# A four-stage transformer kernel on one core: the norms take the next group's scales earlier, and the experts' weight loads wait for the first two tiles' rows

## The chip, the cores and the metric

The kernel runs on one core of a Trainium2 chip, as one program in one launch. The metric is the time of one execution on the device in microseconds (us), lower is better. The kernel before took 1563.83 us (median of three runs, 1562.64 to 1567.59).

## What is computed

The input x is 4 x 512 tokens of width 256. Four layers follow one another, each adding its result to x: attention, a mixture of experts, a state space layer, and the same mixture of experts again. All start with a norm over the 256 features.

```python
def _layernorm(x, axis=-1, eps=1e-05):
    m = jnp.mean(x, axis=axis, keepdims=True)
    v = jnp.var(x, axis=axis, keepdims=True)
    return (x - m) / jnp.sqrt(v + eps)
...
x = x + attention(_layernorm(x))
x = x + ffn(_layernorm(x))
x = x + state_space(_layernorm(x))
x = x + ffn(_layernorm(x))
...
gate_weights = jax.nn.softmax(x @ Wg + bg); topv, topi = jax.lax.top_k(gate_weights, 2)   # 8 experts
h = gelu(x @ W1[n] + b1[n]); h = gelu(h @ W2[n] + b2[n]); eo = h @ W3[n] + b3[n]          # 512, 512, 256 wide
out = sum over the two experts n of a token of topv * eo
```

## The kernel before, in words

x stays in the on-chip memory (SBUF) as X, 16 blocks of 128 tokens. Each layer is made of stages; a stage is one block of five engine programs with a barrier at its end, so a stage can start only when every engine has finished the one before. Inside a stage the order of work on an engine is the order of the code, and the engines meet through semaphores. Float32 products are made of three float16 products (high x high, high x low, low x high, lines 115 to 117), so every operand is first split into a high and a low half.

**Two of the four norms** (before attention, stage "ln0", and before the state space layer, stage "ln2") are made by layer_norm_stage. They run over G = 4 groups of four blocks. For a group g, VectorE takes the statistics (lines 182 to 187), ScalarE the root (line 223), VectorE the reciprocal, the shift and one of the four normalised blocks (normalise, lines 191 to 198), ScalarE the other three blocks (line 232), TensorE turns the group with eight transposes (line 262), ScalarE copies the high half (line 238, copy_turned) and VectorE subtracts the low half (line 204, low_turned). "alongside" is other work put between: in ln0 the splitting of the attention's weights, ScalarE line 144 and VectorE line 149; in ln2 a few steps on ScalarE (line 1494) and most of it on GpSimd (lines 1502 and 1505). Before the change VectorE's loop runs, for each g: normalise(g), statistics(g + 2), low_turned(g - 1), alongside(g).

**The mixture of experts** (ffn_stage, run twice, "ffn1" and "ffn2") makes its own norm and the routing, and then walks over 24 tiles, 15 of 256 rows and 9 of 128 rows, each of one expert. The rows of a tile are gathered from memory by GpSimd with one indirect DMA for 128 rows (line 1033); xs_loaded[0] counts those of even tiles, xs_loaded[1] those of odd tiles, 16 for each DMA, so that 32 means the two gathers of a wide tile. Gathers 0 and 1 (two DMAs each) are started as soon as the row numbers are there (from_ready). The weights of a tile are 2 MB in split form (W); eight tiles' weights fit at once. SyncE asks for them in the order of tiles: for tile 0 in two parts, W1 (512 KB, line 1000, semaphore first_in) and the rest (1.5 MB, line 1001), then one load for each tile (line 1003); from tile 8 on a load waits until tile j - 8 is done (y_psum). The first eight tiles' weights are therefore asked for within 10 us of the start.

TensorE (lines 1110 to 1177) begins with: transpose tile 0's rows (line 1116), layer 1 of tile 0, transpose tile 1's rows; then for each tile layer 2, the next tile's layer 1, the transposes of the tile after that, and layer 3. Layer 1 of tile 0 waits for first_in and for the split rows; layer 2 of tile 0 waits for the 1.5 MB; layer 1 of tile j waits for tile j's 2 MB.

Of the kernel before, what the change touches and what calls it, by code (L numbers as in the profile page):

```python
# [155 lines left out]
def layer_norm_stage(nc, stage, X, XTh, XTl, identf, make_alongside):  # L156

    G = NT // TB  # L160
    with ExitStack() as ctx:
        t = Tensors(nc, ctx, stage)
        stats, mv = t.sb("stats", [P, NT, 6]), t.sb("mv", [P, NT, 2])
        sd, rs, shift = t.sb("sd", [P, NT]), t.sb("rs", [P, NT]), t.sb("shift", [P, NT])
        ring = t.sb("ring", [P, 2, TB, D])
        alongside = make_alongside(t)
        bank = t.banks()
        ordered = t.sem("ordered")
        var_ready, sd_ready, scale_ready = t.sem("var_ready"), t.sem("sd_ready"), t.sem("scale_ready")
        norm_dve, norm_act = t.sem("norm_dve"), t.sem("norm_act")  # L170
        xpose_ready, high_ready, low_ready = (t.sem(n) for n in ("xpose_ready", "high_ready", "low_ready"))
        block = t.block()
        tok = lambda g: slice(g * S, (g + 1) * S)
        tiles_of = lambda g: slice(g * TB, (g + 1) * TB)

        @block.vector
        def _(dve):
            link = Chain(dve, ordered)

            def statistics(g):  # L180
                for n in range(g * TB, g * TB + TB):
                    last = dve.bn_stats(stats[:, n, :], X[:, n, :])
                link(last)
                for n in range(g * TB, g * TB + TB):
                    last = dve.bn_aggr(mv[:, n, :], stats[:, n, :])
                link(last)
                dve.tensor_scalar(mv[:, tiles_of(g), 1], mv[:, tiles_of(g), 1], EPS, None, ALU.add).then_inc(var_ready, 1)

            def normalise(g):
                dve.wait_ge(sd_ready, g + 1)  # L190
                link(dve.reciprocal(rs[:, tiles_of(g)], sd[:, tiles_of(g)]))
                dve.scalar_tensor_tensor(shift[:, tiles_of(g)], mv[:, tiles_of(g), 0], -1.0, rs[:, tiles_of(g)], ALU.mult,
                                         ALU.mult).then_inc(scale_ready, 1)
                if g >= 2:

                    dve.wait_ge(xpose_ready, KD * (g - 1))
                n = g * TB
                dve.tensor_scalar(ring[:, g % 2, 0, :], X[:, n, :], mv[:, n, 0:1], rs[:, n:n + 1], ALU.subtract,
                                  ALU.mult).then_inc(norm_dve, 1)

            def low_turned(g):
                for k in range(KD):
                    dve.wait_ge(high_ready, g * KD + k + 1)
                    dve.tensor_tensor(XTl[:, k, tok(g)], bank[g % 2 * KD + k][:, :], XTh[:, k, tok(g)],
                                      ALU.subtract).then_inc(low_ready, 1)

            statistics(0)
            statistics(1)
            for g in range(G):
                normalise(g)  # L210
                if g + 2 < G:
                    statistics(g + 2)
                if g >= 1:
                    low_turned(g - 1)
                alongside.vector(dve, g)
            low_turned(G - 1)
            alongside.vector(dve, G)

        @block.scalar
        def _(act):  # L220
            def root(g):
                act.wait_ge(var_ready, g + 1)
                act.activation(sd[:, tiles_of(g)], mv[:, tiles_of(g), 1], ACT.Sqrt).then_inc(sd_ready, 1)

            def normalise(g):
                act.wait_ge(scale_ready, g + 1)
                if g >= 2:

                    act.wait_ge(xpose_ready, KD * (g - 1))
                for i in range(1, TB):  # L230
                    n = g * TB + i
                    last = act.activation(ring[:, g % 2, i, :], X[:, n, :], ACT.Identity, scale=rs[:, n:n + 1], bias=shift[:, n:n + 1])
                last.then_inc(norm_act, 1)

            def copy_turned(g):
                for k in range(KD):
                    act.wait_ge(xpose_ready, g * KD + k + 1)
                    act.activation(XTh[:, k, tok(g)], bank[g % 2 * KD + k][:, :], ACT.Copy).then_inc(high_ready, 1)

            root(0)  # L240
            root(1)
            for g in range(G):
                normalise(g)
                if g + 2 < G:
                    root(g + 2)
                if g >= 1:
                    copy_turned(g - 1)
                alongside.scalar(act, g)
            copy_turned(G - 1)
            alongside.scalar(act, G)  # L250

        @block.tensor
        def _(pe):
            for g in range(G):
                pe.wait_ge(norm_dve, g + 1)
                pe.wait_ge(norm_act, g + 1)
                if g >= 2:

                    pe.wait_ge(low_ready, KD * (g - 1))
                for k in range(KD):  # L260
                    for i in range(TB):
                        ins = pe.transpose(bank[g % 2 * KD + k][:, i * P:(i + 1) * P], ring[:, g % 2, i, k * P:(k + 1) * P],
                                           identf[:, :])
                    ins.then_inc(xpose_ready, 1)

        @block.sync
        def _(sp):
            alongside.sync(sp)

        @block.gpsimd  # L270
        def _(pool):
            alongside.gpsimd(pool)
# [601 lines left out]
def ffn_stage(nc, stage, ins, X, split_w, xn_rows, y_rows, row_moves, c, out):  # L874
# [6 lines left out]
    G, C = NT // TB, UNITS  # L881
    PAIR = TOPK * NT
    identf = c["identf"]
    with ExitStack() as ctx:
# [56 lines left out]
        xs_loaded, y_stored = row_moves  # L941
# [13 lines left out]
        def units_of(j, par):  # L955

            return sum(units(i) for i in range(par, j + 1, 2))
# [9 lines left out]
        def expert_of(eng, j):  # L967

            return eng.value_load(tile_expert[0:1, j:j + 1], min_val=0, max_val=NE - 1)

        def tile_weights(j):

            return W[:, j % NE * 2 * WCOLS:(j % NE + 1) * 2 * WCOLS]
# [4 lines left out]
        @block.sync  # L978
        def _(sp):
            sp.dma_start(wg[:, :, :], ins["L0_ffn_Wg"].rearrange("(k p) n -> p k n", p=P)).then_inc(loaded, 16)  # L980
            sp.dma_start(bg[:, :], ins["L0_ffn_bg"].unsqueeze(0).broadcast_to([P, NE])).then_inc(loaded, 16)

            for g in range(G):
                sp.wait_ge(norm_dve, g + 1)
                sp.wait_ge(norm_act, g + 1)
                sp.dma_start(packed_rows(xn_rows[1:, :], g), XN[:, g * TB:(g + 1) * TB, :]).then_inc(xn_stored, 16)
            for layer in range(2):
                sp.dma_start(b12[:, layer, :], ins[f"L0_ffn_b{layer + 1}"].rearrange("e (m p) -> p (e m)", p=P),
                             allow_slow_non_contiguous=True).then_inc(biases, 16)
            sp.dma_start(b3b[:, :, :], ins["L0_ffn_b3"].unsqueeze(0).broadcast_to([P, NE, D])).then_inc(biases, 16)  # L990
            sp.wait_ge(tiles_ready, 1)
            for j in range(NTILE):
                src = split_w[ds(expert_of(sp, j), 1), :, :].rearrange("e p n -> p (e n)")
                if j >= NE:

                    sp.wait_ge(y_psum, j - NE + 1)
                if j == 0:
                    halves = lambda a: a.rearrange("p (x n) -> p x n", x=2)
                    to, src = halves(tile_weights(0)), halves(src)
                    sp.dma_start(to[:, :, 0:W2_AT], src[:, :, 0:W2_AT]).then_inc(first_in, 16)  # L1000
                    sp.dma_start(to[:, :, W2_AT:], src[:, :, W2_AT:]).then_inc(weights[0], 16)
                else:
                    sp.dma_start(tile_weights(j), src).then_inc(weights[j % NE], 16)

            for par in range(2):
                sp.wait_ge(y_stored[par], 16 * units_of(NTILE - 1, par))
            for k, g in BACK:
                sp.dma_start(back[:, k * G + g, :, :], packed_rows(y_rows[1 + k * B * S:, :], g)).then_inc(back_loaded[k * G + g], 16)
# [1331 lines left out]
```

## Time and profile before

| | |
|---|---|
| time, median of 3 runs | 1563.83 us (1562.64 to 1567.59) |
| the profiled execution's own time | 1557.24 us |
| its span from first to last instruction | 1555.5 us |
| TensorE busy | 1230.6 us, 79% of the span |
| VectorE busy | 1003.2 us, 64% |
| ScalarE, GpSimd busy | 617.3 and 621.2 us, 40% each |
| mean granted TensorE clock | 0.897 |
| stage ln0 | from 11.3 to 39.3 us |
| expert loop of ffn1: first gather | 483.07 us |
| stage ln2 | from 741.9 to 766.0 us |
| expert loop of ffn2: first gather | 1293.34 us |

Times of day in the text are us from the start of the span. The 40 slices of the page, in tenths, show TensorE near full through attention and both expert loops, and short valleys at the norms and routings:

```profile
PE   1789898989844999994456869888888846999992
PEclk8799999999965999997578968999999966999997
```

The second line is the TensorE clock granted, in tenths. An execution is a row of stages, so a stretch in which TensorE stands still in a valley goes straight into the time, while a stretch in which another engine waits inside an expert loop doesn't.

### The profile page before, as it was taken

The page shows a single profiled execution, that of the slowest core. Times are in us where ns is not written, and L with a number is a line of the kernel's source. Part 1 is how long each engine was busy: PE and PEld are TensorE (multiplying, and loading weights), DVE is VectorE, ACT ScalarE, POOL GpSimd, SP SyncE. Part 2 cuts the span into 40 slices and gives each one's busy share as a digit, 9 for nine tenths or more (in the row PEclk, how much of TensorE's full clock was granted, in tenths as well). Part 3 has the DMA queues.
Part 4 walks back from the last instruction along what each step waited for, and adds up shares of the span by engine and source line. Part 5 has one row for each costly group of instructions (what it writes and reads, how often), then busy time and mean ns, then how long its engine had stood idle before and what let it go on. Part 6 is the DMA issues. An engine that isn't in the chain of part 4 may idle for free. (4 is left out here: it accounts for less than half of the span.)

```text
span 1555.5 us, 35259 instructions
## 1 busy us (share of the span) xinstructions
PE 1230.6 (79%) x13688; PEld 936.0 (60%) x13688; DVE 1003.2 (64%) x2108; ACT 617.3 (40%) x1380; POOL 621.2 (40%) x540
## 2 busy tenths in 40 slices
PE   1789898989844999994456869888888846999992
PEld 1356665656533989883223436666666634898882
DVE  5478898888865555465586555766666465554565
ACT  4357676666641333342455631121111132333341
POOL 0245445454502333232304345775757502333322
PEclk8799999999965999997578968999999966999997
DMA  4656656666425976643100000000000036967634
GB/s 147 146 136 160 182 166 159 175 162 168 126 60 221 421 289 234 249 163 122 54 1 14 1 14 2 2 3 2 3 2 2 2 83 271 421 247 257 220 142 172
DMA packets 93701, 209.89 MB, mean 135 GB/s; under 512 B 33058, under 2 KB 64547, under 8 KB 87395
## 3 DMA queue, kind: packets, MB, share of 16 engines
q1 hardware_dynamic: 83938, 185.11, 36.4%
q0 software_dynamic: 7488, 20.46, 3.8%
q8 instruction: 109, 1.79, 0.5%
q10 hardware_dynamic: 2112, 2.10, 0.4%
q14 instruction: 54, 0.43, 0.1%
HBM read 152.84 MB, written 37.49 MB: 122 GB/s over the span
## 5 line engine op out<-in xcount | busy, mean ns | idle before, releaser
L1221 ACT ACTIVATE ffn_h<-ffn_bank,ffn_b 128x256 f32<-128x256 f32 (+1 forms) x384 | 144.7, 431 | 271.7 <-PE ffn_bank L117 268.6
L2190 POOL TENSOR_TENSOR ssm_GL<-ssm_L,ssml_G 128x512 f32<-128x512 f32 x128 | 164.9, 1298 | 109.5 <-DVE ssm_L L2099 109.5
L1398 DVE CAST ffn_hh<-ffn_h 128x512 f16<-128x512 f32 (+1 forms) x192 | 73.1, 381 | 185.9 <-ACT ffn_h L1221 185.1
L1033 POOL DMA_INDIRECT ffn_xs<-xn_rows,ffn_from_rows x78 | 78.5, 1007 | 271.2 <-PE ffn_bank L1116 184.7
L115 PE MATMUL ffn_bank<-ffn_hh,ffn_W 128*128 128x256 f16 (+1 forms) x768 | 180.2, 253 | 5.2 <-DVE ffn_hl L1400 5.0
L116 PE MATMUL ffn_bank<-ffn_hl,ffn_W 128*128 128x256 f16 (+1 forms) x768 | 180.0, 252 | 0.0
L117 PE MATMUL ffn_bank<-ffn_hh,ffn_W 128*128 128x256 f16 (+1 forms) x768 | 180.0, 252 | 0.0
L1955 PE MATMUL ssm_Y<-ssm_GL,ssmh_windows 64*32 64x64 f32 x4096 | 145.9, 224 | 8.6 <-POOL ssm_GL L2190 8.2
L2099 DVE TENSOR_TENSOR_SCAN ssm_L<-ssm_bank,ssmh_ident 128x512 f32<-128x512 f32 x128 | 151.2, 1209 | 1.7 <-PE ssm_bank L1938 1.6
L1955 PEld LDWEIGHTS ssm_Y<-ssm_GL,ssmh_windows 64*32 64x32 f32 x4096 | 125.0, 111 | 37.4 <-issue 25.8
L641 ACT ACTIVATE att_prob<-att_bank,att_nmax 128x512 f32<-128x512 f32 (+3 forms) x256 | 127.4, 526 | 29.8 <-DVE att_nmax L723 28.5
L730 DVE TENSOR_TENSOR att_ptl<-att_bank,att_pth 128x384 f16<-128x384 f32 (+1 forms) x192 | 114.0, 594 | 33.9 <-ACT att_pth L648 33.8
L2029 ACT ACTIVATE ssmh_windows<-ssml_dtx 128x64 f32<-128x64 f32 x128 | 32.7, 256 | 259.3 <-PE ssm_Y L1955 255.6
L648 ACT ACTIVATE att_pth<-att_bank 128x384 f16<-128x384 f32 (+1 forms) x192 | 101.5, 529 | 76.7 <-PE att_bank L588 76.7
L588 PE MATMUL att_bank<-main_identf,att_prob 128*128 128x128 f32 x640 | 99.2, 280 | 34.4 <-ACT att_prob L641 19.7
L1040 POOL DMA_INDIRECT y_rows<-ffn_y,ffn_to_rows x78 | 77.1, 988 | 122.3 <-DVE ffn_y L1409 87.0
L723 DVE TENSOR_REDUCE att_nmax<-att_bank 128x1 f32<-128x512 f32 (+3 forms) x256 | 117.6, 479 | 10.6 <-PE att_bank L578 10.3
L833 POOL TENSOR_TENSOR att_rope<-att_turned 128x512 f32<-128x512 f32 x36 | 45.7, 1269 | 193.4 <-DVE att_turned L768 134.9
L1400 DVE TENSOR_TENSOR ffn_hl<-ffn_h,ffn_hh 128x512 f16<-128x512 f32 (+1 forms) x192 | 113.8, 593 | 6.6
L588 PEld LDWEIGHTS att_bank<-main_identf,att_prob 128*128 128x128 f32 x640 | 71.8, 143 | 55.4 <-ACT att_prob L641 41.3
L115 PE MATMUL ffn_bank<-ffn_xTh,ffn_W 128*128 128x256 f16 (+1 forms) x384 | 92.4, 257 | 3.4 <-DVE ffn_xTl L1391 3.4
L116 PE MATMUL ffn_bank<-ffn_xTl,ffn_W 128*128 128x256 f16 (+1 forms) x384 | 92.3, 257 | 0.0
(348 smaller groups left out, 3186.3 us busy)
## 6 DMA issues: line engine op xcount, KB each, us to landing
ffn_W<-split_w SPq DMA_DIRECT2D x46, 2048.0 KB, 10.4
att_piece<-in_ffn_w SPq DMA_DIRECT2D x32, 512.0 KB, 5.4
split_w<-att_halves SPq DMA_DIRECT2D x32, 512.0 KB, 4.4
att_Q<-att_pair SPq DMA_DIRECT2D x64, 128.0 KB, 2.4
ffn_back<-y_rows SPq DMA_DIRECT2D x16, 512.0 KB, 7.2
att_KB<-att_krl SPq DMA_DIRECT2D x8, 512.0 KB, 5.5
att_Q<-att_pair SPq DMA_DIRECT2D x64, 64.0 KB, 2.1
xn_rows<-ffn_XN SPq DMA_DIRECT2D x8, 512.0 KB, 2.6
```

The lines of the kernel that those rows point to most:

```text
L115: pe.matmul(out, ah, bh, start=start, stop=False)
L116: pe.matmul(out, ah, bl, start=False, stop=False)
L117: return pe.matmul(out, al, bh, start=False, stop=stop)
L588: ins = pe.transpose(bk[:, j * P:(j + 1) * P], prob[:, g % 2, at + j * P:at + (j + 1) * P], identf[:, :])
L641: ins = act.activation(prob[:, g % 2, p_at[i]:p_at[i] + n], bank[bk][:, at:at + n], ACT.Exp, bias=nmax[:, g % 2, i:i + 1])
L723: ins = dve.tensor_reduce(nmax[:, g % 2, i:i + 1], bank[bk][:, at:at + (i + 1) * P], AX.X, ALU.max, negate=True)
L730: dve.tensor_tensor(ptl[:, g % 2, at:at + n], bank[5 + (3 * g + c) % 2][:, 0:n], pth[:, g % 2, at:at + n], ALU.subtract).then_inc(pT_low, 1)
L1221: ins_ = act.activation(h[layer][:, m, 0:n], bank[1 + 2 * layer + u][:, (m % 2) * n:(m % 2 + 1) * n], ACT.Gelu, bias=bias[:, ds(e + m, 1)])
L1400: dve.tensor_tensor(hl[layer][:, half, 0:n], h[layer][:, half, 0:n], hh[layer][:, half, 0:n], ALU.subtract).then_inc(h_low[layer], 1)
L1955: ins = pe.matmul(Y[out_rows, q // 2 * 2 + par, q % 2, i, :], windows[rows, p % WINDOWS, x, i, at:at + GROUP], GL[rows, p % RING, x, i, :] ...
L2099: dve.tensor_tensor_scan(flat(L[:, p % RING, :, :, :]), bank[p % 2][:, :], ident8[:, :], 0.0, ALU.mult, ALU.add).then_inc(scan_done, 1)
L2190: pool.tensor_tensor(GL[:, p % RING, :, :, :].rearrange("p x i n -> p x (i n)"), L[:, p % RING, :, :, :].rearrange("p x i n -> p x (i n)") ...
```

## The change

It has two parts. In layer_norm_stage VectorE normalises group 0 ahead of its loop and then, in the turn of g, group g + 1, after the statistics of g + 2 and ahead of low_turned(g - 1) and of the work alongside. ScalarE, TensorE, SyncE and GpSimd keep their programs. In the expert loops SyncE waits for both gathers of tile 0 before it asks for the 1.5 MB of tile 0's weights, and for both gathers of tile 1 before it asks for tile 1's weights and those of later tiles. No other DMA, wait or instruction is added or removed.

```diff
             statistics(0)
             statistics(1)
+            normalise(0)
             for g in range(G):
-                normalise(g)
                 if g + 2 < G:
                     statistics(g + 2)
+                if g + 1 < G:
+                    normalise(g + 1)
                 if g >= 1:
                     low_turned(g - 1)
                 alongside.vector(dve, g)
...
                     sp.dma_start(to[:, :, 0:W2_AT], src[:, :, 0:W2_AT]).then_inc(first_in, 16)
+                    sp.wait_ge(xs_loaded[0], 32)
                     sp.dma_start(to[:, :, W2_AT:], src[:, :, W2_AT:]).then_inc(weights[0], 16)
+                    sp.wait_ge(xs_loaded[1], 32)
                 else:
                     sp.dma_start(tile_weights(j), src).then_inc(weights[j % NE], 16)
```

## Rows read from the trace of the kernel before

**Rows 1.** Waits of TensorE over the whole span: us in total, times, longest

```profile
PE ln_bank L262 <- ACT ln_ring L232: 67.5, 8, 29.9
PE ffn_bank L1116 <- DMA ffn_xs<-xn_rows,ffn_from_rows: 18.2, 2, 9.2
```

**Rows 2.** Timeline of ln0: start, duration, engine, line, what [idle before <- releaser]

```profile
21.11 1.29 DVE L204 TENSOR_TENSOR attw_XTl<-ln_bank,attw_XTh 128x512 f16<-128x512 f32 x2 [0.76 <-ACT attw_XTh L238]
...
23.39 2.29 DVE L149 TENSOR_TENSOR attw_wrl<-ln_staged,attw_wrh 128x2048 f16<-128x2048 f32 x1 [1.00 <-ACT attw_wrh L144]
25.60 2.29 DVE L149 TENSOR_TENSOR attw_wtl<-ln_staged,attw_wth 128x2048 f16<-128x2048 f32 x1
...
28.20 1.58 ACT L232 ACTIVATE ln_ring<-main_X,ln_shift,ln_rs 128x256 f32<-128x256 f32 x3 [3.05 <-DVE ln_shift L192]
...
30.30 1.29 DVE L204 TENSOR_TENSOR attw_XTl<-ln_bank,attw_XTh 128x512 f16<-128x512 f32 x2 [1.81 <-ACT attw_XTh L238]
...
31.83 1.36 DVE L149 TENSOR_TENSOR attw_wxl<-ln_staged,attw_wxh 128x1152 f16<-128x1152 f32 x1 [0.25 <-ACT attw_wxh L144]
...
36.20 1.29 DVE L204 TENSOR_TENSOR attw_XTl<-ln_bank,attw_XTh 128x512 f16<-128x512 f32 x2 [1.81 <-ACT attw_XTh L238]
```

**Rows 3.** Timeline of ln2, the rows that decide its end

```profile
749.67 6.00 POOL L1502 TENSOR_TENSOR ssml_zs<-ssml_zs 128x1344 f32<-128x1344 f32 x2 [16.70 <-DMA ssml_zs<-in_L_attn_b_mup_vector]
...
750.78 1.94 DVE L187 TENSOR_SCALAR ln_mv<-ln_mv 128x4 f32<-128x4 f32 x1
...
754.89 0.80 DVE L192 SCALAR_TENSOR_TENSOR ln_shift<-ln_mv,ln_rs 128x4 f32<-128x4 f32 x1
...
755.73 1.58 ACT L232 ACTIVATE ln_ring<-main_X,ln_shift,ln_rs 128x256 f32<-128x256 f32 x3 [1.79 <-DVE ln_shift L192]
...
759.43 1.58 ACT L232 ACTIVATE ln_ring<-main_X,ln_shift,ln_rs 128x256 f32<-128x256 f32 x3
...
763.26 2.73 POOL L1505 TENSOR_TENSOR ssmi_wil<-ssml_zs,ssmi_wih 128x1344 f16<-128x1344 f32 x1 [0.95 <-ACT ssmi_wih L1494]
```

**Rows 4.** Timeline of the start of the expert loop in ffn1

```profile
484.08 0.67 SPq L1000 DMA_DIRECT2D ffn_W<-split_w  x1
...
484.52 0.95 POOL L1033 DMA_INDIRECT ffn_xs<-xn_rows,ffn_from_rows  x1 [0.30 <-issue]
...
491.46 1.09 PE L1116 MATMUL ffn_bank<-main_identf,ffn_xs 128*128 128x128 f32 x4 [9.18 <-DMA ffn_xs<-xn_rows,ffn_from_rows]
...
494.23 0.37 PE L115 MATMUL ffn_bank<-ffn_xTh,ffn_W 128*128 128x256 f16 x1 [1.69 <-DVE ffn_xTl L1391]
...
501.60 0.27 PE L115 MATMUL ffn_bank<-ffn_hh,ffn_W 128*128 128x256 f16 x1 [1.92 <-DVE ffn_hl L1400]
...
506.83 0.27 PE L115 MATMUL ffn_bank<-ffn_xTh,ffn_W 128*128 128x256 f16 x1
```

**Rows 5.** Line 1033, 483 to 483.5 us: issue to landing of gather one

```profile
DMA to landing us min/median/max: 3.1/3.1/3.1
```

**Rows 6.** Line 1033, 484.4 to 485 us: the same of gather two

```profile
DMA to landing us min/median/max: 6.8/6.8/6.8
```

**Rows 7.** Line 1033, 487 to 487.5 us: the same of gather four

```profile
DMA to landing us min/median/max: 7.9/7.9/7.9
```

**Rows 8.** Gather queue (q0): packets, MB, share; 487 to 488, then 488 to 489

```profile
q0 software_dynamic: 2, 0.01, 5.6%
...
q0 software_dynamic: 20, 0.07, 31.7%
```

**Rows 9.** DMA issues 483 to 500 us: size, issue to landing

```profile
ffn_W<-split_w SPq DMA_DIRECT2D x1, 1536.0 KB, 10.7
```

**Rows 10.** Line 1003, tile 1's load alone, at 486.3 us: issue to landing

```profile
DMA to landing us min/median/max: 14.9/14.9/14.9
```

**Rows 11.** Line 1003, all 46 loads of 2 MB: issue to landing

```profile
DMA to landing us min/median/max: 8.1/10.4/41.7
```

**Rows 12.** Busy time 494.2 to 498.8: PE, PEld, DVE, ACT, POOL, PE clock, DMA share, GB/s

```profile
494.20:498.80 4.60, 4.57 (x22) 3.21 (x23) 0.00 (x0) 1.72 (x3) 0.81 (x1) 0.50 1.00 417
```

## The prediction

> **What bounds the kernel now.** I read the page's busy times and slices first: TensorE is busy for 79% of the span and close to full inside attention and the expert loops, so nothing that another engine does there can shorten the whole unless TensorE is kept waiting. The waits of TensorE say where it stands still. Two entries belong to this change. In the two reordered norms it waits 67.5 us for the normalised blocks, of which 29.9 us is one wait that begins before ln2 [rows 1]; and for the gathered rows at the start of an expert loop it waits 18.2 us, 9.2 at most, two times in all [rows 1], once in ffn1 and once in ffn2. The timelines of these three places then show which engine's work ends last there. In ln0 it is VectorE: it works without pause but for the gaps in brackets, the second low half starts at 30.30 and the third at 36.20, each after 1.81 us of idleness [rows 2]. In ln2 it is the pair of ScalarE and GpSimd, whose last product starts at 763.26 and takes 2.73 us [rows 3]. At the start of the expert loop it is the second gather: issued at 484.52, and TensorE's transposes begin at 491.46 [rows 4, 6].
>
> **Part 1, ln0: 4.5 us off.** Nothing is added or removed; normalise(2) and normalise(3) move ahead of low_turned(0) with the weights' split behind it, and of low_turned(1) with its split. normalise(1) has the same place as before, so all is unchanged up to VectorE's fourth statistics. There VectorE idles 0.76 us before the first low half at 21.11 [rows 2]. normalise(2), 0.7 us of small operations on VectorE, goes into that gap: 0.62 us gained, as 0.14 is left. The two big splits follow; the wait of 1.00 us before 23.39 is for ScalarE's first split [rows 2], which is not moved, so it stays. The second split starts at 25.60 and ends about 27.8. ScalarE meanwhile has had the scales of group 2 since 21 us and need not idle its 3.05 us before 28.20 [rows 2]: it normalises group 2 right after its own splits, at about 25.1 to 26.6, and copies group 1's high half by 27.6. VectorE does normalise(3) at 27.8 and finds that high half ready at 28.4: the gap of 1.81 before 30.30 goes. The 0.25 before 31.83 goes too, as ScalarE has the next split done at 28.7 and VectorE comes at 29.6. TensorE turns group 2 at 26.7 to 28.7, ScalarE normalises group 3 behind its small splits from 29.2 and copies group 2's high half by 31.7, and VectorE, busy to 31.5, goes on without the second 1.81, before 36.20 [rows 2]. What is late next is VectorE's own work, with no gap of note left; TensorE's turn of group 3, 30.8 to 32.7, and the copies to 33.4 are just in time. Sum: 0.62 + 1.81 + 0.25 + 1.81 = 4.49, all of it on the path, since the barrier waits for the last low half. The bounds are 3.0, if the copies of group 3 come a step late, and 4.8.
>
> **Part 1, ln2: nothing.** The same move, but here GpSimd runs two products of 6.00 us together from 749.67 on, 3.0 each [rows 3]. VectorE's little addition of the fourth group, which takes 0.17 us elsewhere, was held for 1.94 us from 750.78, to the end of the first product, and its shift for 0.80 from 754.89, to the end of the second at 755.67 [rows 3]. In the new order normalise(2) comes right behind that addition, at 752.7, when the second product has just begun. Its reciprocal can run but its shift would be held to 755.7, exactly where it ends today; ScalarE's blocks start at 755.73 again [rows 3] and the low half of group 0 is pushed from 753.5 to 756.0, ready at 757.3, when TensorE needs it. Group 3's blocks on ScalarE have no idle time ahead of them at 759.43 [rows 3]: ScalarE was busy with the weights, so earlier scales change nothing. I take 0; the bounds are 0.3 lost and, if the shift slips in before the second product, the 1.79 us that ScalarE idles before 755.73 [rows 3]. The Trainium skill (SBUF — State Buffer, "Who interferes with whom") says that VectorE and GpSimd share a pair of ports, that a VectorE instruction with two SBUF inputs or in a two-port mode takes it, and that whoever issues first keeps it for its whole instruction while the other blocks. The two stretched rows agree; a norm that was free of this rule would give the 1.79.
>
> **Part 2, the expert loops: 2.2 us off each.** Today SyncE asks for 512 KB at 484.08 and, 0.9 us later, for 1.5 MB, and then tile 1's weights at 486.3, while GpSimd issues four gathers 1.2 us apart. The first gather landed 3.1 us after its issue, the second 6.8, the fourth 7.9 [rows 5 to 7]. The second sets when TensorE begins. What of its 3.7 extra us goes away? The wait takes the 1.5 MB and all behind it out of its way, but not the 512 KB. Of the gathers' packets 2 moved from 487 to 488 and 20 from 488 to 489 [rows 8]; so the second gather hardly moved until 3.5 us after its issue, while the 512 KB were in the engines, and I leave that delay in. From then on it shared the engines with the 1.5 MB up to 491.3. Alone, with its descriptors written, it should need no more than the 1.9 us that the first gather took from the end of its instruction (1.2 of the 3.1) to landing [rows 5]. So it lands between 488.8 and 489.7, I take 489.1: 2.2 us. The bounds are 0 (the sharing was not the cause) and 3.7 (the second is as fast as the first). The transposes, the split and layer 1 move with it: layer 1 then starts at 492.0 instead of 494.23, layer 2 at 499.4 instead of 501.60, tile 1's layer 1 at 504.6 instead of 506.83 [rows 4]. ffn2's rows are the same within 0.3 us at all these places, so 2 x 2.2 = 4.4.
>
> **What the new waits hold.** Behind them on SyncE's queue are the weight loads only. The 1.5 MB are issued at 489.2 instead of 484.9. Lag today is 10.7 us with the 512 KB ahead and tile 1's load behind [rows 9]; a load of 2 MB took 8.1 at best and 10.4 in the median [rows 11]. So it lands between 497 and 499.9, against a need at 499.4: cover of about 2 us, at worst 0.5 short. The second wait ends when gather four lands: it was issued at 487.0, and with the engines free of the 1.5 MB until about 490.7 it lands at 490 to 491; at worst at its present 494.9 [rows 7]. Tile 1's load follows 0.8 us later (the read of its expert's number), at 491.5, and lands by the 8.1 to 10.4 at 499.6 to 501.9, behind the 1.5 MB for some of it, against a need at 504.6. Later tiles need theirs 10.9 us apart and the queue delivers one in about 5. So the waits are hidden, with a cover of some 3 us that the present order doesn't need. The Trainium skill (DMA: Bandwidth & Descriptors, "Anatomy of one DMA") speaks against such waits: a DMA costs about 2.0 us fixed, mostly completion, plus its bytes at 436 GB/s, and a wait on a completion exposes the fixed part. By it the 1.5 MB would take 5.6 us and tile 1's load 6.8, which is an estimate from that page and would land both in time.
>
> **The clock.** Layer 1 of tile 0 runs at a granted clock of 0.50, which is 1.2 GHz, after TensorE stood for 9.2 us [rows 12, 1], with 22 products in 4.6 us. It idles 7 us instead and I expect it to be as slow. When the clock rises against the work can shift by a couple of us at either start and at attention's; at half speed half of that is lost or won. I put 1 us on either side.
>
> **Sum.** 4.5 + 0 + 4.4 = 8.9 us. The profiled execution would go from 1557.24 to 1548.3. It was 6.6 us faster than the median of the runs, 0.4%, which is an offset of the run and not of the kernel, so I take the saving from the median: 1563.8 - 8.9 = 1554.9, or 0.57% less.
>
> **Rivals.** (a) More: the second gather becomes as fast as the first, 2 x 3.7, and ln2 gives its 1.8: 13.7 us, 1550.1. For it: the engines had room from 487 to 488, so something other than the 512 KB may have held the second gather, and that would be the 1.5 MB's descriptors. Against: the packets of rows 8. Chance 0.15. (b) The sharing costs the gather little. DMA engines move 417 GB/s in all [rows 12], 26 each, so one 6 KB packet costs 0.23 us, and the gather has three or so packets in each engine: 0.7 us if it waits for one of them each time. Then the loops give 0 to 0.7 each and the sum is 4.5 to 5.9: 1559.3 to 1557.9. The Trainium skill (DMA: Bandwidth & Descriptors, "Queues, rings and completion order") says that each engine goes round robin between its queues, packet by packet, which is this case. Against: a gather in the loads' shadow took 6.8 to 7.9 and not 3.8. Chance 0.2. (c) ln0 doesn't follow, as the copies of groups 2 and 3 come late and half of it is lost: 2 us less, 1557. Chance 0.05. (d) Slower: the second wait ends only at 494.9 and tile 1's load then takes today's 14.9 us [rows 10], landing at 510.6 against 504.6; TensorE waits 6.0, less the 2.2 gained, so 3.8 lost in each loop, 7.6 less ln0's 4.5: 3.1 slower, 1566.9. It decides from the point where tile 1's weights land later than 506.8, 15.3 us after an issue at 491.5. Against: the 14.9 hold the 512 KB and the 1.5 MB that are ahead of it, which by then are done or nearly. Chance 0.04. That the change does nothing at all would need both (b) and (c), and is in them.
>
> **How the numbers follow.** The forecast has a chance of 0.56, 1553 to 1557 by its own bounds. The range takes in (a), (b) and (c), with 1 us for the clock and 1.5 for the medians: 1549.5 to 1562. A difference of 0.3%, 4.7 us, is about what a measurement here can tell from none. The forecast, (a), (c) and the upper half of (b) are faster by more: 0.79; the rest of (b), with some runs of (c), is 0.17; slower by more than that is only part of (d) and a bad clock: 0.04.
>
> **What the new profile would show.** In ln0: no gap before VectorE's low halves but the first and the one before the big split, ScalarE without its 3.05 us, the stage's end at 34.8 in place of 39.3. In ln2: ScalarE's third group at 755.7 less the shift of the start, and the end unmoved. In the loops: TensorE's wait for the gather down from 9.2 to 7, the second gather's lag from 6.8 to 4.6, no idle time before layer 2 of tile 0 or layer 1 of tile 1 put down to a weight load. A lag of 6 or more, or a wait for ffn_W, would prove me wrong; a lag near 3 would be (a).

## The result, and the profile after

| | before | after |
|---|---|---|
| median, six runs each | 1563.75 us (1562.64 to 1567.59) | 1555.84 us (1552.65 to 1559.88) |
| ratio | | 0.9948, 95% interval 0.9931 to 0.9965 |
| the profiled execution's own time | 1557.24 us | 1555.88 us |
| its span | 1555.5 us | 1554.1 us |
| mean granted TensorE clock | 0.897 | 0.901 |

The change takes 7.9 us off, 0.52% with an interval of 0.35 to 0.69%; 8.9 had been forecast. The two profiled executions differ by 1.4 us only. That is not the change's worth: the profile of before was a short execution of its kernel, and the last section says what made it short. So the places are compared first, and the sums after.

On the page of after the busy times and slices look as they did (lines of TensorE and of its granted clock, in tenths). A saving of half a per cent can't be seen here:

```profile
PE   2698898989745999994346869888888846999992
...
PEclk9899999999965999997578968999999966999996
```

TensorE's waits, the answer to [rows 1] (us in total, times, longest), show both parts of the change at once. The normalised blocks cost 62.5 us instead of 67.5, with ln2's 30 among them as before, and the gathers 13.7 instead of 18.2:

```profile
PE ln_bank L264 <- ACT ln_ring L234: 62.5, 8, 30.0
...
PE ffn_bank L1120 <- DMA ffn_xs<-xn_rows,ffn_from_rows: 13.7, 2, 7.2
```

**ln0**, the timeline of after (start, duration, what, [idle before <- releaser]), the answer to [rows 2]:

```profile
21.14 1.29 DVE L204 TENSOR_TENSOR attw_XTl<-ln_bank,attw_XTh 128x512 f16<-128x512 f32 x2 [0.16 <-ACT attw_XTh L240]
...
23.42 2.29 DVE L149 TENSOR_TENSOR attw_wrl<-ln_staged,attw_wrh 128x2048 f16<-128x2048 f32 x1 [1.00 <-ACT attw_wrh L144]
25.08 1.57 ACT L234 ACTIVATE ln_ring<-main_X,ln_shift,ln_rs 128x256 f32<-128x256 f32 x3
...
28.44 1.28 DVE L204 TENSOR_TENSOR attw_XTl<-ln_bank,attw_XTh 128x512 f16<-128x512 f32 x2
...
31.50 1.28 DVE L204 TENSOR_TENSOR attw_XTl<-ln_bank,attw_XTh 128x512 f16<-128x512 f32 x2
...
33.30 1.28 DVE L204 TENSOR_TENSOR attw_XTl<-ln_bank,attw_XTh 128x512 f16<-128x512 f32 x2
...
35.29 0.59 PE L115 MATMUL att_bank<-attw_XTh,attw_wxh 128*128 128x512 f16 x1 [2.59 <-PEq L76]
```

The gap of 0.76 before VectorE's first low half is 0.16, the 1.00 before the big split stands, and the low halves at 28.44 and 31.50 start with no idle time where there were 1.81 us each. ScalarE does group 2's blocks at 25.08 with none of its 3.05 us. Attention's first product comes at 35.29 instead of 39.99.

**ln2**, the answer to [rows 3]. What VectorE gained in place it lost again while GpSimd's products ran:

```profile
750.25 6.00 POOL L1506 TENSOR_TENSOR ssml_zs<-ssml_zs 128x1344 f32<-128x1344 f32 x2 [16.53 <-DMA ssml_zs<-in_L_attn_b_mup_vector]
...
751.13 2.17 DVE L187 TENSOR_SCALAR ln_mv<-ln_mv 128x4 f32<-128x4 f32 x1
...
753.41 2.85 DVE L192 SCALAR_TENSOR_TENSOR ln_shift<-ln_mv,ln_rs 128x4 f32<-128x4 f32 x1
...
756.29 1.58 ACT L234 ACTIVATE ln_ring<-main_X,ln_shift,ln_rs 128x256 f32<-128x256 f32 x3 [1.78 <-DVE ln_shift L192]
```

The shift, 0.16 us elsewhere, takes 2.85 and ends with GpSimd's second product, at 756.25; ScalarE idles 1.78 us before the third group, as it idled 1.79. From ln2's first transpose to the state space layer's first product it is 21.10 us, against 20.93. Over all the profiles below whose GpSimd products are whole, the mean is 21.0 us in six of the new order and 21.1 in six of the old.

**The start of the expert loop in ffn1**, the answer to [rows 4] (SPq are SyncE's requests):

```profile
483.36 0.67 SPq L1002 DMA_DIRECT2D ffn_W<-split_w  x1
483.81 0.95 POOL L1037 DMA_INDIRECT ffn_xs<-xn_rows,ffn_from_rows  x1 [0.30 <-issue]
...
488.80 1.08 PE L1120 MATMUL ffn_bank<-main_identf,ffn_xs 128*128 128x128 f32 x4 [7.24 <-DMA ffn_xs<-xn_rows,ffn_from_rows]
488.82 0.58 SPq L1004 DMA_DIRECT2D ffn_W<-split_w  x1
...
490.30 7.10 SPq L1007 DMA_DIRECT2D ffn_W<-split_w  x7
...
491.57 0.37 PE L115 MATMUL ffn_bank<-ffn_xTh,ffn_W 128*128 128x256 f16 x1 [1.69 <-DVE ffn_xTl L1395]
...
498.97 0.10 PEld L115 LDWEIGHTS ffn_bank<-ffn_hh,ffn_W 128*128 128x128 f16 x1 [2.74 <-DMA ffn_W<-split_w]
499.00 0.37 PE L115 MATMUL ffn_bank<-ffn_hh,ffn_W 128*128 128x256 f16 x1 [2.53 <-DVE ffn_hl L1404]
```

The second gather is issued at 483.81 and TensorE starts on its rows at 488.80, 5.0 us later, where it was 6.9 [rows 4]. The 1.5 MB are asked for at 488.82 and have landed when layer 2 wants them. The weight load at 498.97 is put down to that DMA and the product 0.03 us behind it to VectorE, because the weight load itself waits for nothing but the DMA. By the semaphores' times in the trace the last part of the 1.5 MB landed at 498.10, and VectorE finished at 498.86. So VectorE ended the wait, and the load had 0.8 us to spare.

### The profile page after: what moved, and what is told of

It is laid out like the page before. It is cut to its first block and busy times, and to the rows that moved or that the text cites. A ratio compares the mean times of both kernels' runs of the same rounds, so it can differ in the third digit from the quotient of the medians.

```text
span 1554.1 us, 35259 instructions
## 1 busy us (share of the span) xinstructions
PE 1234.1 (79%) x13688; PEld 936.3 (60%) x13688; DVE 1006.2 (65%) x2108; ACT 616.6 (40%) x1380; POOL 621.4 (40%) x540
## 3 DMA queue, kind: packets, MB, share of 16 engines
q8 instruction: 109, 1.79, 0.5%
```

## The experiments

All of them are set against the kernel before on the same chip. Times of after's and before's profiles scatter by some us in attention, so single places are read in the profiles and kernels are compared by ratios. Each ratio is followed by its 95% interval.

### The norms alone

```diff
+            normalise(0)
             for g in range(G):
-                normalise(g)
                 if g + 2 < G:
                     statistics(g + 2)
+                if g + 1 < G:
+                    normalise(g + 1)
```

> The norms' new order alone, no new waits in the expert loops. My theory: ln0 ends 4.5 us earlier and ln2 gives nothing, because VectorE's shift of group 2 is held by GpSimd's second product (2 to 3 us in its row); the gathers keep their 6.8 us lag. Time 4.5 us less than before (ratio 0.997). Rival one, that the norms carry the whole saving: 8 us less. Rival two, that later stages give ln0's saving back, since TensorE's clock in attention falls more often when it starts earlier: 0 to 1 us less.

Measured: 1558.97 us against 1562.39, 0.9966 (0.9951 to 0.9981), which is 5.3 us. Its ln0 took 17.94 us from the first transposes to attention's first product, before's 22.68.

### Both waits alone, the first alone, the second alone

```diff
                     sp.dma_start(to[:, :, 0:W2_AT], src[:, :, 0:W2_AT]).then_inc(first_in, 16)
+                    sp.wait_ge(xs_loaded[0], 32)
                     sp.dma_start(to[:, :, W2_AT:], src[:, :, W2_AT:]).then_inc(weights[0], 16)
+                    sp.wait_ge(xs_loaded[1], 32)
```

> The two waits of SyncE alone, the norms in their old order. My theory: the second gather lands 4.7 to 5.0 us after its issue in place of 6.8, TensorE's wait for the rows falls from 18.2 to about 13.7 us over both loops, and the time is 4.4 us less (ratio 0.997), with 1 us either way from when the clock rises. Rival, that the late loads or the clock take it back (a wait for ffn_W, or a fall to 1.2 GHz inside layer 1 or 2 of tile 0): the same wait for the rows, but 0 to 1.5 us less.

> Only the first wait: the 1.5 MB of tile 0 wait for tile 0's rows, tile 1's load follows at once; norms in their old order. My theory: tile 0's rows land as with both waits, since all that shares with them is behind the first wait, so TensorE's wait for the rows is about 13.7 us in all and the time is as in the kernel with both waits, 4.4 us less; gathers three and four may land later by 1 to 3 us, which costs nothing because TensorE asks for them 7 us later. Rival, that holding tile 1's load back is what helps: no better than before.

> Only the second wait: the 1.5 MB are asked for at once as before, tile 1's load and those behind it wait for tile 1's rows; norms in their old order. My theory: the 1.5 MB alone share with the second gather, whose lag stays at 6.5 to 6.8 us, and the time is that of the kernel before within 1 us. Rival, that the number of loads queued behind matters (descriptors of several loads being made while the gather's are fetched): lag 5 to 6 us and 1 to 3 us less.

Measured: both 0.9972 (0.9959 to 0.9985), the first 0.9973 (0.9958 to 0.9988), the second 0.9997 (0.9982 to 1.0011); in us 4.4, 4.2 and 0.5. TensorE's wait for the gathers in the profiles of the two waits, of the first and of the second:

```profile
PE ffn_bank L1118 <- DMA ffn_xs<-xn_rows,ffn_from_rows: 13.9, 2, 7.1
```

```profile
PE ffn_bank L1117 <- DMA ffn_xs<-xn_rows,ffn_from_rows: 14.4, 2, 7.4
```

```profile
PE ffn_bank L1117 <- DMA ffn_xs<-xn_rows,ffn_from_rows: 18.5, 2, 9.6
```

All three came as the first theory of each had it. What follows: the loops' gain is the first wait's. The second neither gives nor costs anything that can be told. The norms' 5.3 and the waits' 4.4 add up to 9.7, against 7.9 to 8.6 of the whole change; the intervals, some 2 us either way each, cover that.

### Before once more, and GpSimd's second product in ln2 cut to 8 columns, in the new order and in the old

```diff
-            pool.tensor_tensor(self.w[:, k, :], self.w[:, k, :], self.mup, ALU.mult).then_inc(self.scaled, 1)
+            n = PROJ if k == 0 else 8
+            pool.tensor_tensor(self.w[:, k, 0:n], self.w[:, k, 0:n], self.mup[:, 0:n], ALU.mult).then_inc(self.scaled, 1)
```

> The kernel before once more, for a second profile of it. In the first one attention took 401.7 us from its first to its last product, and the step from tile 17's transposes to tile 18's took 5.9 us in both expert loops; in the kernel after these are 405.8 us and 7.2 us. One theory: both are luck of an execution and not of the change, so a second profile shows attention anywhere from 401 to 407 us and the step at 7.2. The other: the old order keeps them short, so it shows 401.7 and 5.9 again.

> The kernel after with GpSimd's second product in ln2 cut from 1344 to 8 columns, which leaves the state space layer's second half of scaled weights out of the computation. My theory: VectorE's shift of group 2, 2.85 us long in the kernel after, falls to 0.2, and ScalarE's blocks of group 2 start 1.2 to 1.8 us earlier, right behind its copy. Rival: the shift is slow for a reason of its own (its operands), stays over 1 us, and nothing moves.

> The kernel before with the same cut (the second half of the scaled weights of the state space layer is left out of the computation). Beside the run above it shows what the new order of the norm is worth in ln2 when nothing holds VectorE: from ln2's first transposes to its last, 0.6 to 1.8 us less in the new order. If the order is worth nothing there at all, both take the same.

Both kernels leave out the scaling of the other columns of the second half. Measured, one execution each: 1552.45 us in the new order, 1562.13 in the old; single executions scatter too much for these two times to be compared, so the timelines are read. The two products together now take 3.19 us in place of 6.00. In the new order:

```profile
749.28 3.19 POOL L1507 TENSOR_TENSOR ssml_zs<-ssml_zs 128x1344 f32<-128x1344 f32 x2 [16.43 <-DMA ssml_zs<-in_L_attn_b_mup_vector]
750.27 2.06 DVE L187 TENSOR_SCALAR ln_mv<-ln_mv 128x4 f32<-128x4 f32 x1
...
752.45 0.16 DVE L192 SCALAR_TENSOR_TENSOR ln_shift<-ln_mv,ln_rs 128x4 f32<-128x4 f32 x1
```

In the old order:

```profile
759.20 0.16 DVE L192 SCALAR_TENSOR_TENSOR ln_shift<-ln_mv,ln_rs 128x4 f32<-128x4 f32 x1
759.39 1.58 ACT L232 ACTIVATE ln_ring<-main_X,ln_shift,ln_rs 128x256 f32<-128x256 f32 x3 [1.15 <-DVE ln_shift L192]
```

The addition is still held to the end of the first product, which was left as it was, and the shift is not held any more: 2.85 us became 0.16 with nothing else in the code changed. From ln2's first transpose to the state space layer's first product it took 19.08 us in the new order and 20.32 in the old, where it was 21.1 with whole products in both. So without the second product the new order would be worth 1.2 us here, by one profile each. It is GpSimd's product that holds VectorE's shift, and it takes about what the change could give in ln2. The Trainium skill (SBUF — State Buffer, "Who interferes with whom") has the rule that of VectorE and GpSimd the one that issues first keeps the shared ports for its whole instruction and the other blocks. The trace agrees with it: with the product there the shift ended when the product did, and without it the shift took 0.16 us.

Before's second profile took 1553.94 us, 3.3 less than its first, with the same code. Its two waits for the gather were 8.07 and 7.96 us. Its attention took 400.69 us and its step from tile 17 to tile 18 took 5.9, as the expectation's second theory had it. That the old order keeps them short was disproved only by later profiles: the run with the cut product in the old order had an attention of 406.00, and before's third profile, below, had 406.07 and a step of 7.1.

### The 512 KB behind the first two gathers as well

```diff
+                    sp.wait_ge(xs_loaded[0], 32)
                     sp.dma_start(to[:, :, 0:W2_AT], src[:, :, 0:W2_AT]).then_inc(first_in, 16)
-                    sp.wait_ge(xs_loaded[0], 32)
                     sp.dma_start(to[:, :, W2_AT:], src[:, :, W2_AT:]).then_inc(weights[0], 16)
```

> The kernel after with the 512 KB of W1 asked for behind the first wait too, so that no weight load runs beside tile 0's gathers. My theory: the 512 KB cost the second gather 1.3 to 1.8 us, so its lag falls from 4.9 to 3.1 to 3.5 us, but W1 then lands 4 to 5 us after that, at about the time at which layer 1 starts now or 1 us later: the same time as the kernel after, within 1.5 us. Rival, that the 512 KB cost it nothing and the second gather is late from its own making: lag still 4.5 or more, layer 1 waits for W1, 2 to 4 us slower than the kernel after.

Measured: 1557.74 us against 1560.9, 0.9981 (0.9963 to 0.9999): 0.0033 worse than after's 0.9948, some 5 us. The timeline of the start in ffn1:

```profile
483.57 0.95 POOL L1037 DMA_INDIRECT ffn_xs<-xn_rows,ffn_from_rows  x1 [0.30 <-issue]
...
486.40 1.09 PE L1120 MATMUL ffn_bank<-main_identf,ffn_xs 128*128 128x128 f32 x4 [5.08 <-DMA ffn_xs<-xn_rows,ffn_from_rows]
486.45 0.67 SPq L1003 DMA_DIRECT2D ffn_W<-split_w  x1
...
493.23 0.39 PE L115 MATMUL ffn_bank<-ffn_xTh,ffn_W 128*128 128x256 f16 x1 [5.74 <-DMA ffn_W<-split_w]
```

and one line of its DMA issues there (size, us to landing):

```profile
ffn_W<-split_w SPq DMA_DIRECT2D x1, 512.0 KB, 6.7
```

The expectation of the same time within 1.5 us missed, although its mechanism on the gather's side came out: 2.8 us from issue to TensorE's start, the time of a gather with no weight load beside it. So of before's 6.9 us in ffn1 the 1.5 MB and what follows took 1.9 and the 512 KB 2.2; by the means over all profiles, 6.45 without the first wait, 4.77 with it and 2.86 here, they took 1.7 and 1.9. The loss is on the other side. The expectation gave the 512 KB 4 to 5 us. SyncE asked for them 0.85 us ahead of the 1.5 MB, and they took 6.7 us, where after's, asked for early, took 5.0. Layer 1 starts 11.1 us after the first gather's issue (482.12), against a mean of 9.0 in the loops with the first wait alone or with both, about 2 us later in each loop; that is 4 of the 5. The 5 compares ratios of two chips and is good to some 4 us either way.

### The 512 KB between the first gather and the second

Two profiles had then shown both ends: asked for early the load slows the gather, asked for late it is late itself. The next kernel gives the first gather a semaphore of its own, and SyncE waits for that one gather before the 512 KB; TensorE waits for both semaphores.

```diff
+        rows0 = xs_loaded[2]
...
+                    sp.wait_ge(rows0, 16)
                     sp.dma_start(to[:, :, 0:W2_AT], src[:, :, 0:W2_AT]).then_inc(first_in, 16)
-                    sp.wait_ge(xs_loaded[0], 32)
+                    sp.wait_ge(xs_loaded[0], 16)
...
-                                            ).then_inc(xs_loaded[j % 2], 16)
+                                            ).then_inc(rows0 if n == 0 else xs_loaded[j % 2], 16)
```

> The kernel after once more, beside the three below on one chip. By the sum of its parts (norms 0.9966, waits 0.9972) the ratio should be 0.994 and by its first timing 0.9948: 8 to 9 us less than before. If attention really runs some 3 us longer when it starts 4.7 us earlier (405.6 to 406.7 us in four profiles of the new order, 400.7 to 406.8 in six of the old one), its profile shows 405 or more again; if that was luck, 401 to 407.

> The kernel after with the 512 KB of W1 held until the first gather has landed (it gets a semaphore of its own). My theory: the second gather's lag falls from 4.9 to 3.0 to 3.7 us, W1 lands 5.0 to 5.5 us after its issue, which is 0.7 to 1.2 us before layer 1 starts now, so 1.5 to 2.4 us less than the kernel after over both loops (ratio to it 0.9985 to 0.999). Rival: W1 lands 6.7 us after its issue as when all loads waited, so layer 1 starts where it does now or 0.5 us later and nothing is gained.

> The norms' new order alone, once more. Theory one: ln0's 4.7 us arrive in full, ratio 0.997, and attention's length in the profile is as scattered as in the old order (401 to 407 us). Theory two: attention gives 2 to 4 us of it back, ratio 0.9985 to 0.9995, with attention at 405 us or more in the profile once more.

> The kernel before, a third profile, to see how attention scatters in the old order and whether the step from tile 17's to tile 18's transposes (5.9 or 7.2 us) goes by the occasion and not by the kernel. If it goes by the occasion it is the same here as in the other kernels of this call.

| on one chip | median us | against before |
|---|---|---|
| after, again | 1554.66 | 0.9945 (0.9929 to 0.9961) |
| the 512 KB later | 1552.88 | 0.9935 (0.9918 to 0.9952) |
| the norms alone, again | 1557.02 | 0.9967 (0.9951 to 0.9982) |
| before, its third profile | 1564.39 (one execution) | (median of the runs 1563.19) |

The start in ffn1 with the 512 KB later:

```profile
479.38 0.95 POOL L1039 DMA_INDIRECT ffn_xs<-xn_rows,ffn_from_rows  x1 [0.30 <-issue]
...
481.08 0.67 SPq L1004 DMA_DIRECT2D ffn_W<-split_w  x1
...
482.24 1.09 PE L1124 MATMUL ffn_bank<-main_identf,ffn_xs 128*128 128x128 f32 x4 [5.10 <-DMA ffn_xs<-xn_rows,ffn_from_rows]
482.26 0.58 SPq L1006 DMA_DIRECT2D ffn_W<-split_w  x1
...
486.03 0.39 PE L115 MATMUL ffn_bank<-ffn_xTh,ffn_W 128*128 128x256 f16 x1 [2.70 <-DMA ffn_W<-split_w]
...
489.24 17.61 SPq L1009 DMA_DIRECT2D ffn_W<-split_w  x8
```

TensorE waits 5.1 us for the gather, no more than with the 512 KB out of the way, and then for the 512 KB, whose wait is 2.70 where VectorE alone would have made it 1.69. Layer 1 starts 8.1 us after the first gather's issue (477.94) in ffn1 and 8.35 in ffn2, against 9.2 and 8.5 in after and 8.8 and 8.6 in after again, so it is 1.1 us sooner at best and 0.1 at least. The gather's lag of 2.9 us to TensorE's start and the 512 KB's 4.9 and 5.2 are close to what the theory had. The median is 1.8 us below after's, also as forecast, but the intervals overlap: that this kernel beats before is shown, that it beats after isn't. It pays elsewhere: tile 1's load is asked for only at 489.24, which fits gathers three and four sharing the DMA engines with the 1.5 MB now (not tested apart), and in ffn2 tile 1's layer 1 had to wait for its weights:

```profile
1299.94 7.00 SPq L1009 DMA_DIRECT2D ffn_W<-split_w  x7
...
1311.43 0.28 PE L115 MATMUL ffn_bank<-ffn_xTh,ffn_W 128*128 128x256 f16 x1 [2.23 <-DMA ffn_W<-split_w]
```

That 2.23 us is the mechanism of the prediction's rival (d), the late second wait, met in a neighbour of this kernel. The profile shows no gain after it: from ffn2's first transpose to the end of the span it took 297.6 us against 294.1 in after again, and what made this profile the shorter one is its attention, 401.44 us against 406.29.

## Why the prediction came out right, and where its sizes were off

**ln0, right.** Forecast 4.49 us in four pieces (0.62, 1.81, 0.25, 1.81), measured 4.70 at attention's first product. VectorE and ScalarE came where the working put them: blocks of group 2 at 25.08 (25.1 said), TensorE's turns at 26.75 and 30.77 (26.7 and 30.8), the last low halves ending at 34.58. That no copy of groups 2 and 3 came late disposes of rival (c). It arrives in full: the norms alone gave 0.9966 and 0.9967, 5.2 us, with 2 to 3 us of uncertainty each.

**ln2, right for the right reason.** Nothing gained, the shift held to the end of the second product, and the cut product shows that some 1.2 us would be there if it weren't; the prediction had put the most at 1.79. Rival (a)'s 1.8 for ln2 falls.

**The loops, right mechanism, the term too large.** The step that was mis-sized is the 2.2 us per loop, and in it the starting value. The profiles with the first wait hold ten waits for the gather (after's two, two more in after again, in the cut product, in both waits, in the first alone): 6.47 to 7.38 us, mean 6.96. Those without it hold fourteen (the three profiles of before, the cut product in the old order, the norms twice, the second wait alone): 7.96 to 9.63, mean 8.63. So a loop gains 1.7 us and an execution 3.35. In before's own first profile the two waits were 9.2 and 9.0 [rows 1], among the longest of the fourteen, and a term read from one execution took that scatter with it: against after's 13.7 the drop looks like 4.5, the forecast's 4.4, which is luck. The second gather came 4.9 us after its issue in after's ffn1, against 4.6 forecast. From its issue to TensorE's start, 0.14 us more, it is 4.77 us in the mean of the ten, which the forecast hit, and 6.45 in the mean of the fourteen, where the forecast had started from 6.9. Rival (b), 0 to 0.7 a loop, is ruled out by the means and by the first wait's 0.9973. Rival (a), a second gather as fast as the first, is ruled out by after's 5.0 against 2.8 once the 512 KB are gone too: the working had left that delay in, on the packets of [rows 8], and it was worth 2.2 us (1.9 by the mean of the four waits with the 512 KB out of the way, 5.05).

**The waits' cover, right in the outcome, one of its two loads mis-sized.** The 1.5 MB were asked for at 488.82 (489.2 said) and landed 9.3 us later, 0.8 us before the need. In the other nine loops with the first wait they took 7.6 to 8.2 us and landed 1.9 to 2.5 us before it; the working had 8 to 10.7 us and a cover of about 2. The Trainium skill (DMA: Bandwidth & Descriptors, "Anatomy of one DMA") had given an estimate of 5.6 us. The traces do not agree: none took less than 7.6. The Trainium skill's fit there is for DMAs that GpSimd issues; these are SyncE's, with gathers three and four and tile 1's load beside them. Which of these matters was not tested.

Tile 1's load was asked for at 490.30 (491.5 said), and no wait of TensorE for it shows in either loop. But it took longer than the 8.1 to 10.4 us of the working: 13.4 us in ffn1 and 10.8 in ffn2 by the semaphores' times, and 10.8 to 13.4 over the ten loops. So the step that took its lag from the run of all 46 such loads had this load's price wrong. What made it longer is open; it shared the DMA engines with the 1.5 MB ahead and the loads behind. The next two lines show the 1.5 MB in ffn1 of the kernel with the cut product in the new order, and tile 1's 2 MB in ffn1 of after again:

```profile
DMA to landing us min/median/max: 7.8/7.8/7.8
```

```profile
DMA to landing us min/median/max: 13.3/13.3/13.3
```

It was hidden in ffn1 because it was asked for 1.2 us sooner than forecast: it landed at 503.72, for a need at 505.62 (504.6 said). The margin was 1.9 and 2.4 us in after, and only 0.7 in ffn1 of the kernel with both waits and the old norms. Rival (d) did not happen here, as its gather four landed at 489.55 and not at 494.9, but its other half, a load of 14.9 us, was nearer to the truth than the working's 10.4. The profile's line that puts 2.74 us before layer 2 down to ffn_W is one of the signs that the prediction had named against itself; VectorE's end 0.76 us after the landing answers it.

**The sum, and the offset.** 4.7 + 0 + 3.35 = 8.05 us, against 7.9 in the medians and, by the ratios 0.9948 and 0.9945, 8.1 and 8.6. The forecast of 8.9 was 1.05 too large in the loops and 0.2 too small in ln0. One of its chances is mis-added: 0.56, 0.15, 0.05 and half of 0.2 make 0.86 and not 0.79; no time hangs on it. Taking the saving from the median and not from the profiled execution was right: before's other profiles took 1553.94 and 1564.39 us, so the 6.6 us were scatter. Two profiles that happen to have the same length of attention, the third of before and the second of after, on one chip, show the whole change, between the same instructions (attention from its first product to the end of its last):

| us | before | after | saved |
|---|---|---|---|
| ln0: first transpose to attention's first product | 22.67 | 17.93 | 4.74 |
| attention | 406.07 | 406.29 | -0.22 |
| ffn1: first transpose to tile 0's transposes | 39.97 | 38.74 | 1.23 |
| ffn1: from there to ln2's first transpose | 258.07 | 259.80 | -1.73 |
| ln2: to the projections | 21.52 | 21.04 | 0.48 |
| projections, state space | 491.22 | 491.18 | 0.04 |
| ffn2: first transpose to tile 0's transposes | 40.06 | 38.39 | 1.67 |
| ffn2: from there to VectorE's last sum | 252.86 | 251.59 | 1.27 |

The sum is 7.5. The -1.73 and the 1.27 come from where TensorE's clock rose. First the stretch from tile 0's transposes to tile 2's in before's third profile, ffn1 and ffn2 (us, busy time of PE, PEld, DVE, ACT, POOL, granted clock, DMA share, GB/s):

```profile
494.80:512.80 18.00, 13.45 (x104) 11.10 (x105) 5.81 (x11) 6.45 (x13) 3.78 (x4) 0.85 1.02 414
1305.70:1325.40 19.70, 15.90 (x105) 12.27 (x106) 5.88 (x11) 6.54 (x13) 4.27 (x4) 0.74 1.02 425
```

and in after's second:

```profile
488.90:508.60 19.70, 15.62 (x105) 12.18 (x106) 5.96 (x11) 6.46 (x13) 3.77 (x4) 0.74 0.96 370
1299.30:1317.60 18.30, 15.08 (x105) 12.09 (x106) 6.00 (x11) 6.56 (x13) 4.03 (x4) 0.76 0.96 368
```

One of the two loops took 1.4 to 1.7 us more in either kernel, ffn2 in before and ffn1 in after. In after's first profile it was ffn1: its clock rose near the end of layer 1, TensorE then idled 2.5 us, and layer 2 ran from its start at 1.2 GHz, a granted clock of 0.50:

```profile
499.00:501.50 2.50, 2.50 (x12) 1.76 (x13) 0.45 (x1) 0.00 (x0) 0.07 (x1) 0.50 1.02 436
```

Among the fourteen loops without the first wait three went so, among the ten with it also three. They lie unevenly: ffn1 in all three profiles with both parts of the change and ffn2 in none of them, ffn2 in three of the seven without the first wait and ffn1 in none. So that the change has no part in it is not shown. The prediction's 1 us either side for the clock was of that size.

## What to carry to other kernels

Where a small transfer decides when a stage begins, try keeping the large ones off the queues until it has landed, but price each large one's own lag first, from loads that run beside the same neighbours. A load asked for late can put its whole lag on the path, as the 6.7 us of the 512 KB did here. A place between two small transfers is worth trying, though the times here don't show that it is better. Work moved ahead of a wait gains just the idle time that the timeline shows before its later steps, so add those up gap by gap, and check whether another engine's long operation holds the moved one. Take a saving's size from several profiled executions when one wait scatters by as much as the saving.

## What was not expected of the hardware

**Attention takes one of two lengths.** From its first product to its last it took 400.5 to 403.0 us in six of the fourteen profiles and 405.6 to 406.8 in eight, with both orders of the norms in both groups (before 401.74 and 406.07, the norms alone 406.50 and 400.51). The granted clock in the windows of before's first and third profile is 0.95 and 0.94, and TensorE's busy time 348 and 353 us:

```profile
39.99:441.73 401.74, 348.07 (x3392) 235.57 (x3392) 322.93 (x822) 246.64 (x521) 186.82 (x136) 0.95 0.58 153
```

```profile
40.10:446.20 406.10, 353.06 (x3392) 237.44 (x3392) 322.96 (x822) 246.27 (x521) 186.71 (x136) 0.94 0.57 151
```

Over the six TensorE's busy time averages 348.7 us and its granted clock 0.954, over the eight 352.8 and 0.941, so some 4.1 of the 4.7 us between the two means are TensorE running at 1.2 GHz for longer. That the new order brings the longer attention is not borne out: it had five of the eight long ones, but the norms alone, once more, had the shortest of all and kept their whole gain. What decides between the two was not tried. It is more than half of what the whole change gives, and explains much of why the first pair of profiles differed by 1.4 us: the lengths 401.74 and 405.77 hide 4.0 of the saving.

**One step of the expert loop is 1.27 us longer in some profiles.** From tile 17's transposes to tile 18's it was 5.9 us in both loops in five profiles (before's first, and all four of the chip that ran the cut product and the early 512 KB test) and 7.1 to 7.3 in the other nine, with both orders of the norms in both groups. On each of the three chips of the experiments the profiles agree, so it goes with the occasion and not with the code; its cause stays open. It costs 2.5 us an execution and is the other thing that made the first pair look alike.

**The same 512 KB took from 4.5 to 6.7 us to land.** Asked for early, with the 1.5 MB 5.0 to 5.7 us behind them, they took 4.5 to 5.2 us in the eight loops where the trace has the landing. With the early order and no first wait, where the 1.5 MB come 0.85 us behind, they took 5.2 to 5.8 in twelve. Between the gathers, with 1.2 us between the two loads, they took 4.9 and 5.2, and behind both first gathers, with 0.85, they took 6.7 in both loops. A load close behind seems to cost them up to 1 us, but that doesn't explain the 6.7; gathers three and four, issued just before them, are what is left, and that was not tried apart.
